# Late rounds of an attention and expert kernel: scores in two halves, U in three passes, softmax by pairs, other places for silu and the mixes

## The reference

```python
xn = layernorm(x)
q, k, v = (xn @ Wq + bq), (xn @ Wk + bk), (xn @ Wv + bv)          # 4 heads x 256
qr, qi, kr, ki = q * cos(phase), q * sin(phase), k * cos(phase), k * sin(phase)
attn = softmax((qr . kr + qi . ki) / 16)                           # over the 4 heads of one token
out = swapaxes(attn @ v, 1, 2).reshape(b, s, h * d)
s = out @ Wo + bo
gates = sinkhorn((xn @ router_w.T + router_b) / temperature)       # 8 experts, 3 iterations
ffn = xn + sum over the top 2 experts of gate * (relu(xn @ wg) * (xn @ wp)) @ wo
result = x + s * silu(ffn)
```

## Time and profile before

| | |
|---|---|
| median of 3 runs | 1589.56 us (1588.63 to 1591.09) |
| the profiled execution | 1596.37 us, its span 1594.6 us |
| TensorE busy | 1533.0 us, 96% |
| VectorE busy | 976.4 us, 61% |
| GpSimd busy | 794.2 us, 50% |
| ScalarE busy | 729.6 us, 46% |
| mean granted clock of TensorE | 0.986 |

### The profile page before, as it was taken

One profiled execution on the slowest core, in us unless ns is written; L12 is line 12 of the kernel. 1 busy time (PEld: TensorE's weight loads), 2 busy tenths in 40 slices (PEclk: granted clock), 3 DMA queues, 4 the chain that ended last, 5 costly groups with the idle time before them and its releaser, 6 DMA issues.

```text
span 1594.6 us, 32793 instructions
## 1 busy us (share of the span) xinstructions
PE 1533.0 (96%) x11408; PEld 1168.2 (73%) x11408; DVE 976.4 (61%) x1880; ACT 729.6 (46%) x1205; POOL 794.2 (50%) x945
## 2 busy tenths in 40 slices
PE   5999699989999999999999999999999999999997
PEld 2546565658888888888888888776666776666774
DVE  7567899953333333333333333577889788888777
ACT  4766334413333333333333333546456565555552
POOL 4637588913344434443344333253584564853456
PEclk9999899989999999999999999999999999999998
DMA  9989842266133232223211231255555666455464
GB/s 326 395 316 331 299 175 72 75 206 209 56 132 96 96 113 76 88 102 112 78 54 57 71 145 44 91 165 176 179 181 180 201 197 226 149 164 168 148 205 146
DMA packets 175351, 251.23 MB, mean 158 GB/s; under 512 B 15336, under 2 KB 122656, under 8 KB 175072
## 3 DMA queue, kind: packets, MB, share of 16 engines
q1 hardware_dynamic: 160576, 211.48, 38.8%
q0 software_dynamic: 12960, 35.41, 6.7%
q10 hardware_dynamic: 1664, 2.26, 0.4%
HBM read 149.58 MB, written 99.50 MB: 156 GB/s over the span
## 4 chain that ended last, share of the span: by engine, by line
PE 90%; DVE 6%; DMA 1%; ACT 1%; issue 1%; SPq 1%; ACTq 0%; DVEq 0%
PE ps L1147 24%; PE ps L1082 21%; PE ps L1093 13%; PE ps L1166 12%; PE ps L1029 7%; PE ps L1156 4%; PE ps L1050 2%; PE ps L1129 2%; PE ps L998 2%; PE ps L926 1%; PE ps L982 1%; PE ps L916 1%; DVE UN L1232 1%; DMA WR<-w_d 1%; DVE OH L1555 1%
## 5 line engine op out<-in xcount | busy, mean ns | idle before, releaser
L1147 PE MATMUL ps<-WR,FR 128*128 x1620 | 407.6, 401 | 2.3 <-DMA WR<-w_d 2.3
L1147 PEld LDWEIGHTS ps<-WR,FR 128*128 128x128 f32 x1620 | 295.8, 189 | 59.9 <-issue 2.5
L651 POOL DMA_INDIRECT y_d<-AUX x135 | 133.3, 987 | 353.0 <-ACT AUX L870 353.0
L1658 DVE TENSOR_TENSOR AUX<-AUX,ps 128x512 f32<-128x512 f32 x135 | 93.0, 689 | 341.2 <-ACT AUX L858 341.2
L819 ACT ACTIVATE WM<-ps,bcs,trig 128x512 f32<-128x512 f32 x256 | 253.1, 1016 | 90.7 <-PE ps L1082 83.4
L1598 DVE TENSOR_SCALAR WM<-ps,vec,trig 128x512 f32<-128x512 f32 x256 | 244.4, 993 | 62.7 <-ACT WM L819 62.0
L1093 PE MATMUL ps<-WM,XTJ 128*128 128x512 f32 x512 | 237.1, 600 | 0.0
L858 ACT ACTIVATE AUX<-ps 128x512 f32<-128x512 f32 x135 | 80.9, 599 | 317.5 <-PE ps L1147 282.8
L1082 PE MATMUL ps<-XH,WH 128*128 128x512 f32 x512 | 205.2, 401 | 4.8 <-issue 3.8
L1166 PE MATMUL ps<-WR,ABR 128*128 x1080 | 209.4, 292 | 0.0
L1082 PE MATMUL ps<-XL,WH 128*128 128x512 f32 x512 | 200.2, 391 | 0.0
(11 more groups left out here) (238 smaller groups left out, 2202.9 us busy)
## 6 DMA issues: line engine op xcount, KB each, us to landing
US<-u_d SPq DMA_DIRECT2D x63, 512.0 KB, 4.8
u_d<-UN SPq DMA_DIRECT2D x120, 256.0 KB, 2.0
WR<-w_d SPq DMA_DIRECT2D x96, 256.0 KB
AUX<-y_d SPq DMA_DIRECT2D x32, 512.0 KB, 5.5
WM<-in_L_attn_x_dram SPq DMA_DIRECT2D x16, 512.0 KB, 9.6
xn_d<-WM SPq DMA_DIRECT2D x32, 256.0 KB, 7.4
w_d<-USR SPq DMA_DIRECT2D x16, 512.0 KB, 4.2
AUX<-xn_d SPq DMA_DIRECT2D x16, 512.0 KB, 6.1
```

Source lines behind the costliest of these rows:

```text
L651: e.indirect_dma_start(y_d, bass.IndirectOffsetOnAxis(toks[:, n:n + 1], 0), YS[n % 4], None).then_inc(s_y[n % 4], 16)
L1147: mm = e.matmul(b[:, :], x, WR[:, bass.ds(off[m] + (2048 * z + 1024 * a + 512 * k), 512)], start=(k == 0 and x is xh and z == 0), stop=(k ...
L1658: e.tensor_tensor(HS[:, m % 2, :], GR[:, :], mP[m % 2][:, :], ALU.mult).then_inc(s_h, 1)
```

## The change

All of it is in the late rounds (q >= 4), but for the split of M.

- **Order of chunks.** First the even chunks (P0: the first half of d of Q and K), U chunks 16 to 19, a new step 24 with the first half of the scores, the odd chunks (P1), U chunks 20 to 23, the second half of the scores. In round 15 all U chunks stand before step 24. The rotated parts take half the room (QH), which the odd chunks write again. Banks are set by two tables (BANKS).
- **U in three passes.** M is split into MH and ML during the experts' stage: ScalarE loads and stores 16 pieces, VectorE splits them, and SyncE loads both near the stage's end. GpSimd copies XH and XL into the order of U (XHJ, XLJ; `xj`) and doesn't add them.
- **Rotations.** ScalarE makes both parts of chunks 10, 11, 14 and 15 (K); VectorE has 12 chunks left.
- **Softmax by pairs** of tiles (soft_a2, soft_b2, spread2).
- **silu.** silu(q-1) at step 24, silu(host) after chunk 20, silu(15) after chunk 5, in P1.
- **Mixes** after c = 19, step 24, c = 21 and 23 (round 15: 19, 20, 23, step 24); the last four stand at the very end. The turn of x after c = 20 and 22.
- x of round 15 is loaded to another place and later (load_x).

```diff
+        P0, P1 = tuple(range(0, 16, 2)), tuple(range(1, 16, 2))
+        def order(q):
+            if q < QE:
+                return tuple(range(24))
+            if q < NQ - 1:
+                return P0 + (16, 17, 18, 19) + P1 + (20, 21, 22, 23)
+            return P0 + tuple(range(16, 24)) + P1
+        def at(q, c):
+            return 24 * q + order(q).index(c) + 1
+        BANKS = {c: (0, 1, 6, 7, 2, 0, 1, 2)[i] for i, c in enumerate(P0)}
+        BANKS.update({c: (1, 2, 6, 7, 0, 1, 2, 0)[i] for i, c in enumerate(P1)})
+        def bank(q, c):
+            if q < QE:
+                return (0, 1, 2, 4, 5)[c % 5] if c < 16 else (c - 15) % 3
+            if q == QE and c in P0:
+                return (0, 1, 4, 5, 2, 0, 1, 2)[c // 2]
             if c < 16:
-                return ((0, 1, 2, 4, 5) if q <= QE else (0, 1, 2, 6, 7))[c % 5]
-            return (c - 15) % 3
-
-        held, prior = {}, {}
-        for g in range(24 * NQ):
-            prior[g] = held.get(bank(g))
-            held[bank(g)] = g
+                return BANKS[c]
+            if q < NQ - 1:
+                return (0, 1, 2, 0, 1, 2, 0, 1)[c - 16]
+            return (c - 16) % 3
+        def steps(q):
+            if q < QE:
+                return order(q)
+            u = 23 if q == NQ - 1 else 19
+            i = order(q).index(u) + 1
+            return order(q)[:i] + (24,) + order(q)[i:]
+        def mixes(q):
+            if q < QE:
+                return {18: 0, 20: 1, 22: 2, 23: 3}
+            return {19: 0, 20: 1, 23: 2, 24: 3} if q == NQ - 1 else {19: 0, 24: 1, 21: 2, 23: 3}
+        def lone(q, c):
+            return q >= QE and c in (10, 11, 14, 15)
+        def turns(q):
+            return {17: 0, 20: 1} if q < QE else {20: 0, 22: 1}
...
+            def xj(q):
+                e.wait_ge(s_xtd, 2 * q + 2)
+                e.wait_ge(s_ch, 24 * q)
+                if q == QE:
+                    e.wait_ge(s_dn, NM)
+                for k in range(2):
+                    for v, w in ((XHJ, XH), (XLJ, XL)):
+                        for j in range(2):
+                            ins = e.tensor_copy(v[:, k, 2 * j:2 * j + 2, :],
+                                                w[:, k, :].rearrange("p (r j) -> p j r", j=4)[:, 2 * j:2 * j + 2, :])
                     ins.then_inc(s_xtj, 1)
...
-                    for c in range(24):
-                        e.wait_ge(s_ch, 24 * q + c + 1)
-                        b = ps[bank(24 * q + c)][:, :]
+                    for c in steps(q):
+                        if c == 24:
+                            if q > QE:
+                                silu(q - 1)
+                            continue
+                        e.wait_ge(s_ch, at(q, c))
+                        b = ps[bank(q, c)][:, :]
                         if c < 16:
                             x, i = c // 8, c % 8
-                            e.activation(rotated(2 * x, i), b,
+                            if lone(q, c):
+                                e.activation(rotated(q, 2 * x + 1, i), b, ACT.Identity, bias=bcs[:, x, 1, i:i + 1],
+                                             scale=trig[:, 1, i:i + 1])
+                            e.activation(rotated(q, 2 * x, i), b,
                                          ACT.Identity, bias=bcs[:, x, 0, i:i + 1],
                                          scale=trig[:, 0, i:i + 1]).then_inc(s_ca, 1)
                         else:
                             w = 8 * q + c - 16
+                            if w == 8 * QE:
+                                e.wait_ge(s_mst, 16 * 16)
...
                             side[24 * q + c]()
-                        if q > QE and c == 18:
-                            silu(q - 1)
-                        if q == NQ - 1 and c == 23:
+                        if q == NQ - 1 and c == 5:
                             silu(q)
-                        if q + 1 < q1 and c in (17, 20):
-                            xt(q + 1, c // 20)
+                        if q in host and c == 20:
+                            silu(host[q])
+                        if q + 1 < q1 and c in turns(q):
+                            xt(q + 1, turns(q)[c])
+                    if q >= QE:
+                        for n in (4 * q, 4 * q + 2):
+                            e.wait_ge(s_sub, n + 2)
+                            e.activation(SE4[:, n % 4:n % 4 + 2, :], SS4[:, n % 4:n % 4 + 2, :], ACT.Exp,
+                                         scale=1.0 / 16).then_inc(s_exp, 2)
+                        continue
...
                                               QT[:, 2 + x, h, :].rearrange("p (g t) -> p g t", g=H)[:, :, col // 4:col // 4 + 16],
                                               start=(x == h == 0), stop=(x == h == 1))
                 mm.then_inc(s_s, 1)
+            def half_scores(q, h):
+                e.wait_ge(s_ca, at(q, 14 + h))
+                e.wait_ge(s_cd, rotated_by[q, 14 + h])
+                if h == 0:
+                    e.wait_ge(s_sm1, 4 * q)
+                for i in range(4):
+                    for c in range(4):
+                        for x in range(2):
...
                             for k in range(2):
-                                mm = e.matmul(b[:, :], XTJ[:, k, a // 2, :], M_s[:, k, 512 * a:512 * a + 512],
-                                              start=(k == 0), stop=(k == 1))
+                                if q < QE:
+                                    mm = e.matmul(b[:, :], XTJ[:, k, j, :], M_s[:, k, cols],
+                                                  start=(k == 0), stop=(k == 1))
+                                    continue
+                                for xx, w in ((XHJ, MH), (XHJ, ML), (XLJ, MH)):
+                                    mm = e.matmul(b[:, :], xx[:, k, j, :], w[:, k, cols],
+                                                  start=(k == 0 and xx is XHJ and w is MH), stop=(k == 1 and xx is XLJ))
...
+                        if q > 0 and c in mixes(q):
+                            if c == (18 if q < QE else 19) or QE <= q < NQ - 1 and c == 21:
+                                last = 15 if q < QE or c == 21 else 14
+                                e.wait_ge(s_ca, at(q, last))
+                                e.wait_ge(s_cd, rotated_by[q, last])
+                            mix(4 * q - 4 + mixes(q)[c])
+                        if q + 1 < q1 and c in turns(q):
+                            xt(q + 1, turns(q)[c])
+                    if q >= QE:
+                        half_scores(q, 1)
+                        continue
                     e.wait_ge(s_ca, 24 * q + 16)
                     e.wait_ge(s_cd, 16 * q + 16)
                     for i in range(4):
...
+                        elif q:
+                            if c == 16:
+                                spread2(n)
+                                biased(n)
+                            elif c == 17:
+                                biased(n + 1)
+                            if c in mixes(q):
+                                mixed(n + mixes(q)[c])
+                                if mixes(q)[c] == 1:
+                                    spread2(n + 2)
+                                    biased(n + 2)
+                            if c == (23 if q == NQ - 1 else 20):
+                                biased(n + 3)
                         if (q, c) in firsts:
                             marks(firsts[q, c])
                         if q - 1 in host and c == 8:
                             early(host[q - 1])
...
+                    if q >= QE:
+                        soft_a2(n)
+                        soft_a2(n + 2)
+                        soft_b2(n)
+                        if q < NQ - 1:
+                            soft_b2(n + 2)
+                            continue
+                        spread2(n)
+                        soft_b2(n + 2)
+                        spread2(n + 2)
+                        for i in range(4):
+                            mixed(n + i)
...
+            def split_m(i):
+                e.wait_ge(s_mr, 16 * (i + 1))
+                ch(e.tensor_copy(UNR[:, 1, :], UN[:, 0, :]))
+                e.tensor_tensor(UNR[:, 2, :], UN[:, 0, :], UNR[:, 1, :].bitcast(F32), ALU.subtract).then_inc(s_msp, 1)
```

More of the change, by code:

```diff
@@ L86, in program @@
         XL = sb("XL", [128, 2, 512], F32R)
+        with nc.sbuf_tensor("XHJ", [128, 2, 4, 128], F32R) as XHJ:
+            pass
         XTJ = sb("XTJ", [128, 2, 4, 128])
+        with nc.sbuf_tensor("UNR", [128, 3, 512], F32R) as UNR:
+            pass
         UN = sb("UN", [128, 3, 512])
@@ L428, in load_c, with load_x @@
                     e.dma_start(xx[h:128:4], rows(xf, q)[h]).then_inc(sl, 16)
+            def load_x():
+                e.wait_ge(s_ch, at(NQ - 1, 17))
+                for h in range(H):
+                    e.dma_start(cs(NQ - 1)[3][h:128:4], rows(xf, NQ - 1)[h]).then_inc(s_xe, 16)
             def load_e(k):
@@ L695, in _ @@
                 if q < NQ:
[L696 removed]
```

(14 more changed lines are left out.)

186 lines of the change are left out of this document (137 added, 49 removed).

## The result

| | before | after |
|---|---|---|
| median of 4 runs | 1590.12 us | 1618.60 us (1614.41 to 1619.45) |
| ratio, 95% interval | | 1.016 (1.014 to 1.018) |
| the profiled execution, its span | 1596.37, 1594.6 | 1619.45, 1617.3 |
| mean granted clock of TensorE | 0.986 | 0.978 |

The change makes the kernel slower, by 1.6%. Forecast were 1594 us and a range from 1573 to 1609: the direction was right, the size was not.

A forecast was written before the change was run, and what follows sets the result against it. It took late rounds, bound by TensorE before, to become locked to the load chain through silu(q-1). Terms -7 + 12 - 2 + 1 = +4 us on a median of 1589.56 gave 1594 us, range 1573 to 1609.

The forecast's parts named there:

- what the rounds are locked to: Rounds 6 to 14: silu(q-1) waits for total and the load chain, 48.8 us a round against 47.5, +12 us.
- TensorE's own work: A late round: 43.4 us from S to S if nothing else came to end later.
- total's length: GpSimd's total in rounds 6 to 14: 11.5 us, with the biased of one mix falling into it.
- Rounds 4 and 5 are free: Total's data lie there long before; each round brings 3.6 us, -7 together.
- from S+2.5, needed at S+14.7: nothing: GpSimd's eight copies of x in place of four additions: 3.5 to 9.4 us in all, no cost.
- U's saving: U chunks of rounds 4 to 15: 1.36 for 1.815 us, 3.6 us a round, 43.7 us in all.
- The tail: From S of round 14 to the end: S+66 to 70 against 71.5 before, taken as -2 us.
- Rival 2 (the clock): Clock falls in each stall of rounds 6 to 14, 1.7 us each unless hidden: 1609 us, chance 0.08.
- chunk 15's wait: P1 of rounds 6 to 14: TensorE idles another 1.85 us before chunk 15, which could hide a clock fall.
- Rival 1 (the load chain gives way): Total ends by S+26.5 and a round takes 43.4 us: 1545, then 1542 us, chance 0.12.
- Smaller edits: Fewer rotations, softmax by pairs, lone chunks, copies of x, M's split and DMAs: 0 to +2, taken as +1 us.
- the lone chunks: ScalarE's K chunks, four a round: 1.56 us against a chunk's 1.36, covered by U chunks behind each pair.

The follow-up runs named there:

- e1: Changed kernel with silu(q-1) of rounds 6 to 14 moved from step 24 to behind U chunk 20: 1589.4 us.
- e8: e7 with a tiny exponential that loads its table early (as e5) and silu(15) behind chunk 15 instead of chunk 5: 1571.4 us.
- e10: The changed kernel run again without any edit: 1612.6 us.
- e4: Changed kernel with U of rounds 4 to 15 in float32 matmuls again, x added up by GpSimd instead of copied: 1614.9 us.
- e11: Changed kernel with GpSimd's eight copies of x per late round replaced by additions of the same part to itself (U doubled): 1611.3 us.
- e2: Changed kernel with GpSimd's copies of x waiting for the end of the softmax of the round before: 1607.5 us.
- e9: e8 with U of the late rounds in float32 matmuls again, GpSimd adding behind the softmax: 1594.3 us.
- e5: Changed kernel with one tiny exponential on ScalarE ahead of its wait for the softmax in each late round: 1610.5 us.
- e7: e3 with silu(host) in rounds 5, 7, 9 and 11 behind U chunk 23 instead of chunk 20: 1571.6 us.
- e3: Changed kernel with the edits of e1 and e2 together: 1587.5 us.

## Why the prediction was wrong

**Right: what the rounds are locked to.** total starts at S+17.6 to S+21.3 in the trace (20.25 forecast), ScalarE passes silu(q-1) only when it has ended, P1 stops, and a round takes 48.9 us (1450.07 to 1498.98; the nine 49.4 in the mean) where 48.8 were forecast. e1 takes that silu away and the stalls of P1 go with it. What the traces don't bear out in it is the balance inside: TensorE's own work is 44.8 (e8), not 43.4, and the stalls are shorter than 5.3. In round 7 P1 doesn't stop at all: it begins late, at S+29.7, behind a pause of 1.82 us in the first half of the scores that no run explains. The nine together took 5.5 us more than forecast (444.7 against 439.2), and the term that was too small is total's length: 11.7 to 13.4 us, 12.4 in the mean, where I had 11.5. That is 0.9 a round, 8 us in all. The other terms came out a little shorter: total's start at S+20.1 in the mean, and from the end of silu to the next S 15.8 us for the forecast's 16.0. The median, 1618.6, lies 24.6 us over the forecast's 1594. What the late stage doesn't explain of that lies before it or is scatter: e10, the same kernel, has 1612.6.

**The step that failed: "Rounds 4 and 5 are free", -7.** They cost +4.5 (1.0 and 3.5), 11.7 of the 18.7 us by which the late stage exceeds the table's forecast. Three parts:
- *7.1 us in round 5.* P0 is 6.1 us longer: TensorE waits 3.16 us, and then runs for some 6 us at half clock (0.50 in both stretches of 2 us from 1066 to 1070). Behind it is VectorE's subtraction of 5.19 us. I had costed the copies of x "from S+2.5, needed at S+14.7: nothing", by when their result is needed and not by what they do to the engine beside them. The earlier trace rows had brought me to one instruction's delay at a time, and the Trainium skill (SBUF — State Buffer, section SBUF: two separate sides), by which the two engines exclude each other for a whole instruction, agreed. Beside additions (e4, e11) the measurement still agrees; beside the copies it doesn't, and there the measurement decides. e2 and e11 each take the 6 us out: 45.1 and 44.4.
- *4.6 us in round 4, of which 3.8 are a slip.* S is the start of the scores before, and of their second half after. In round 4 the first half, 3.8 us, comes ahead of it. I carried S over without adding it.
- *U's saving.* 0.455 us a chunk came from one pair of chunks that begins behind another unit (3.63 us), where four in a row take 6.95 (e9). 2.8 us a round in the changed kernel (e4) and not 3.6, which is the rest of what rounds 4 and 5 lack. In the nine locked rounds it is worth 2 to 3 us together, as e4 shows.

**The tail, -2: -0.5.** The wait behind silu(15) came as described: 2.55 and 1.54 us. So did the clock. TensorE's busy us, granted clock, DMA share and GB/s in stretches at the changed kernel's end:
```profile
1597.00:1599.00 2.00, 1.95 (x36) 0.50 0.48 156
...
1605.00:1607.00 2.00, 0.00 (x0) 0.99 0.00 0
1607.00:1609.00 2.00, 1.63 (x16) 0.50 0.00 0
```
Behind each pause it is 0.50 (1.2 GHz), and the last half scores take 5.33 us instead of 3.95.

**Rival 2 (the clock) came true in part.** In round 6, right behind P1's stop of 2.69 us:
```profile
1138.00:1140.00 2.00, 0.82 (x2) 0.69 (x3) 2.00 (x3) 2.00 (x3) 1.78 (x3) 0.83 0.00 0
1140.00:1142.00 2.00, 2.00 (x6) 1.58 (x5) 2.00 (x4) 1.44 (x3) 0.00 (x0) 0.50 0.00 0
```
In the first profile the clock fell behind the stops of 2.69, 2.83, 2.70 and 2.39 us (rounds 6, 8, 10, 12) and not behind those of 1.75, 1.69 and 1.51 (rounds 9, 11, 13). But the fall costs far less than the rival's 1.7 us. From the end of silu(q-1) to the next S it is 15.9 to 16.1 us in the four rounds with a fall and 15.5 in rounds 9, 11, 13 and 14, which have none: 0.55 each, 2.2 us in all. The rest is hidden as the prediction's rival itself allowed, under chunk 15's wait. Where the clock stayed at 1.00, TensorE stops a second time, as in round 9:
```profile
1291.06 0.47 PE L1241 MATMUL ps<-XH,WH 128*128 128x512 f32 x1 [0.72 <-ACT WM L926]
```
Where it fell, that second stop is gone. Rounds 6, 8, 10 and 12 took 50.3 us in the mean and rounds 7, 9, 11 and 13 49.0, but they are also the rounds behind a host round, where silu(q-1) ended at S+34.2 in the mean and not at S+33.3; that makes the larger part of the difference. In e10 the clock fell in seven of the nine rounds, and stayed low longer in rounds 9 and 10 (17.2 and 17.5 us from silu to S), yet the nine took 444.0 us together, for total was shorter there, 11.9 us.

**Rival 1 (the load chain gives way)** didn't come: ScalarE waited for GpSimd in all nine rounds, 55.5 us in sum (in the host rounds 7, 9 and 11 only 1.9 to 3.9 each, since it had stood 5.1 to 6.3 us before that for the writes of U). The waits of the changed kernel from 1100 to 1560 us (engine, line, what it waited for: us, times, longest):
```profile
POOL AUX L762 <- DMA AUX<-in_L_attn_x_dram: 118.6, 9, 14.4
...
ACT L949 <- DVE AC L1703: 61.9, 10, 6.9
...
ACT AUX L906 <- POOL AUX L769: 55.5, 9, 8.7
```
But the time that the rival named, 1545, was also out of reach: with the stalls of P0 and P1 gone (e8) it is 1571.

**"Smaller edits", +1.** M's split shows no cost (the first chunk of round 4 stands at 1009.4 us before and at 1004.3 to 1010.7 in the changed kernels), and the lone chunks show one for certain in round 15 only, the wait of 1.54 us; the copies of x are told above. The exponential's table load behind its wait was no item of the list at all, and costs 3 to 4 us of the late stage (e5).

**Where the expected gain went.** U's matmuls save 23 us (e9 against e8). The changed kernel gives them back and 21 more: silu(q-1) in ScalarE's queue 23 (e1), the copies beside the softmax 7 to 8 (e2), silu(host) ahead of the turn, which shows only once the first is mended, 12 (e7 against e3), silu(15) 3. The terms overlap and don't add up; taken away together, with the table load, they give 606 - 563 = 43.

## What to carry to other kernels

An instruction that waits for another engine's chain belongs at a place of its queue where nothing behind it is on the path; ask it of each such instruction again when the order changes, for mending the worst one uncovers the next (silu(q-1), then silu(host)). A faster unit is worth little in rounds that are locked to a chain beside it: the same edit of U brought 0 us in one kernel (2 to 3 in its locked rounds, less what its copies cost) and 23 us in the other, so test it on the kernel whose stalls are gone. And cost an operation that is moved beside another engine by what it does to that engine's shortest instruction too, not only by when its result is needed.

## What the runs showed of the hardware

- **GpSimd's copies can shut out a two-input operation of VectorE for many instructions.** A 128x32 subtraction in SBUF, 0.19 us alone, took 3.00 us beside back-to-back casts of 0.6 us, or 5.19 across the last cast and eight products behind it. Of 24 subtractions eight took over 2 us in one profile and one in the next (e10), where the others took 0.68 at most beside the same casts. Beside additions of the same length (0.62 us, e11) it took 0.72 at most. Why the 5.19 reach over products, which are no copies, no run tells apart. The prediction's one lost instruction at a time holds for additions here, and for copies only in some of their meetings.
- **A table load can stand on either side of its first instruction's wait.** In the changed kernel silu's (1.28 us) was ahead of the wait in each of the rounds 6 to 14 (in round 6 ahead of one of 8.38 us); the exponential's was behind it each time, after 4.5 to 6.9 us. An exponential without a wait, put in front, moved the load ahead (1590.39 in e5, right behind the last rotation); what decides it otherwise wasn't tried.
- **TensorE's clock fell behind the longer stops, not behind each.** It was 0.50 (1.2 GHz) behind stops of 2.4 to 3.2 us and 1.00 (2.4 GHz) behind those of 1.5 to 1.75 in the same kernel. In e10 it fell behind one of 2.08 us (round 14), and not behind one of 2.82 (1131.78), so the length alone doesn't decide. A fall in a round that waits for another chain cost 0.55 us, since the slower matmuls took the place of a wait.
